# Expert layer of a decoder block: 39 padded tiles gathered and scattered, or 32 dense tiles read by 39 slots and summed in SBUF

## What is computed

```
logits = xf @ w_router.T                  # 2048 tokens x 8 experts
topw, topi = top_k(softmax(logits), 2)    # two experts for each token
topw = topw / sum(topw)
down_e = (silu(xf @ w_gate[e].T) * (xf @ w_up[e].T)) @ w_down[e].T
out = x + sum over its two experts of topw * down_e
```

## Time and profile before

| | |
|---|---|
| median of 3 runs | 475.76 us (475.4 to 476.47) |
| the profiled execution, its own time | 476.23 us |
| its span in the profile | 474.4 us |
| share of the span that PE / DVE / ACT / POOL are busy | 89% / 68% / 61% / 44% |
| mean granted clock of PE | 0.963 of full |

### The profile page before, as it was taken

One profiled execution on the slowest core, in us unless ns is written; L12 is line 12 of the kernel. 1 busy time (PEld: TensorE's weight loads), 2 busy tenths in 40 slices (PEclk: granted clock), 3 DMA queues, 4 the chain that ended last, 5 costly groups with the idle time before them and its releaser, 6 DMA issues. The chain is left out here.

```text
span 474.4 us, 13915 instructions
## 1 busy us (share of the span) xinstructions
PE 422.3 (89%) x4047; PEld 341.0 (72%) x4047; DVE 324.8 (68%) x969; ACT 291.1 (61%) x868; POOL 206.4 (44%) x482
## 2 busy tenths in 40 slices
PE   3989999999999999999988899987988999999950
PEld 3567777777777677777766687887877888888840
DVE  5579888888888888888885688888762333333325
ACT  4678888888888888888875877642022323323224
POOL 1545455454554554555531110100014777777740
PEclk9999999999999999999998999999778999999985
DMA  6363111111111111111000000001017766666526
GB/s 181 74 226 126 34 34 43 33 35 42 33 44 33 33 44 33 34 44 33 11 2 1 0 2 1 1 1 68 23 33 240 216 210 197 210 208 202 190 59 240
DMA packets 31999, 38.86 MB, mean 82 GB/s; under 512 B 5952, under 2 KB 29184, under 8 KB 31712
## 3 DMA queue, kind: packets, MB, share of 16 engines
q1 hardware_dynamic: 29040, 33.33, 22.9%
q0 software_dynamic: 2496, 5.12, 3.4%
q10 hardware_dynamic: 432, 0.02, 0.1%
HBM read 33.80 MB, written 4.65 MB: 81 GB/s over the span
## 5 line engine op out<-in xcount | busy, mean ns | idle before, releaser
L397 ACT ACTIVATE PR<-PS,nmax 128x257 f32<-128x257 f32 x256 | 117.9, 474 | 32.8 <-DVE nmax L582 32.7
L582 DVE TENSOR_REDUCE nmax<-PS 128x1 f32<-128x257 f32 x256 | 90.5, 416 | 17.5 <-PE PS L872 16.7
L879 PE MATMUL PS<-I,PR 128*128 128x128 f32 x512 | 67.3, 275 | 0.0
L346 POOL DMA_INDIRECT XG<-x_table,IDX x39 | 37.9, 971 | 57.4 <-DVE IDX L796 45.8
L879 PEld LDWEIGHTS PS<-I,PR 128*128 128x128 f32 x512 | 58.6, 142 | 0.3 <-issue 0.3
L300 POOL TENSOR_TENSOR O<-OM 128x64 f32<-128x64 f32 x64 | 20.4, 319 | 85.6 <-DVE OM L605 85.6
L802 DVE TENSOR_TENSOR H<-PS,SG 128x384 f32<-128x384 f32 x39 | 21.8, 558 | 50.9 <-PE PS L1089 50.9
L397 ACT ACTIVATION_READ_ACCUMULATOR PR<-PS,nmax 128x1 f32 x256 | 52.0, 203 | 0.0
L527 ACT ACTIVATE SG<-PS 128x384 f32<-128x384 f32 x39 | 19.1, 490 | 50.3 <-PE PS L1089 50.3
L894 PE MATMUL PS<-PT,KV 128*32 128x128 f32 x1024 | 41.6, 280 | 7.0 <-DVE PT L587 6.2
L872 PE MATMUL PS<-KV,QM 32*128 32x257 f32 x512 | 45.8, 427 | 1.3 <-ACT PR L397 0.7
(11 more groups left out here) (190 smaller groups left out, 836.5 us busy)
## 6 DMA issues: line engine op xcount, KB each, us to landing
CR<-ctxT SPq DMA_DIRECT2D x64, 128.0 KB, 2.1
GC<-w_gate SPq DMA_DIRECT2D x39, 192.0 KB, 2.7
UC<-w_up SPq DMA_DIRECT2D x39, 192.0 KB, 3.1
Y<-y_table SPq DMA_DIRECT2D x4, 512.0 KB, 5.1
DW<-w_down SPq DMA_DIRECT2D x1, 1536.0 KB, 6.0
NAMES<-lanes SPq DMA_DIRECT2D x1, 1344.0 KB, 9.1
X<-x SPq DMA_DIRECT2D x4, 256.0 KB, 4.6
x_table<-xe SPq DMA_DIRECT2D x4, 256.0 KB, 2.4
```

Source lines behind the costliest of these rows:

```text
L397: a.activation(PR[:, j % 2, gr, 0:S], src, ACT.Exp, bias=bias, accum_out=rsum[:, j % 2, gr:gr + 1]).then_inc(exped, 1)
L582: v.tensor_reduce(nmax[:, gr:gr + 1], bank[gr][:, 0:S], AX.X, ALU.max, negate=True).then_inc(max_ready, 1)
L879: ins = t.transpose(bank[4 + ch][:, 128 * gr:128 * gr + 128], PR[:, j % 2, gr, KC * ch:KC * ch + KC], I128[:, :])
```

## The change

The padding goes away. The 4096 pairs are sorted by expert without gaps, so they fill exactly `LT` = 32 tiles; a tile in which an expert ends and another begins belongs to both. The loop runs over `SLOTS` = 32 + 8 - 1 = 39 slots, each a pair of (tile, expert): the slot's expert comes out of `packed` as before, and its tile is the slot's number less the expert's (`tile_of`).

- POOL gathers 32 tiles and scatters 32. `XG` has 20 places, so 20 gathers come first; then gather t+20 and scatter t in turn, while gathers last, and scatters alone after that. Scatter t waits until slot t+7 is summed. Eight semaphores go round among the gathers.
- `XGT` keeps all 32 turned tiles, so gate and up read it at an address out of a register.
- A slot computes all 128 rows of its tile. DVE sets the rows of other experts to zero on the way out of PSUM (`own_rows`, a maximum and a minimum against `least` and `most` of that slot), and adds the tile to `YA` in SBUF (`added`), whose place is also an address out of a register. POOL zeroes `YA` beforehand. The scatter reads `YA`.
- The masks `least` and `most` are nine more instructions on DVE, behind `IDX` and ahead of the loop. DVE now also loads the five packed words into registers.
- The routing loses five DVE instructions (`over` to `base`) and the padding's `empty`; the places come out of PE ready for use. One `keep_busy` has 5 matmuls in place of 10.
- The two turns of tiles 0 and 1 both come ahead of the first gate product; after that a slot turns tile s+2.

```
-TILES = (2 * B * L + E * 127) // 128
-XRING, YRING, WRING = 4, 4, 4
+LT = 2 * B * L // 128
+SLOTS = LT + E - 1
+XRING, GRING, WRING = 20, 8, 4
...
-        owner_steps = 19
+        owner_steps = 13
         def owners_of(engine):
             _, words = nc.values_load_multi_w_load_instructions(packed[0:1, :], engines=[engine],
                                                                 min_val=0, max_val=E ** PER_WORD - 1)
-            return [((words[s // PER_WORD] >> (3 * (s % PER_WORD))) & (E - 1)) * IP for s in range(TILES)]
+            return [((words[s // PER_WORD] >> (3 * (s % PER_WORD))) & (E - 1)) for s in range(SLOTS)]
...
-            for n in range(YRING):
-                sp.wait_ge(scattered[n], 16 * len(range(n, TILES, YRING)))
+            sp.wait_ge(scattered, 16 * LT)
...
-            def gather(s):
-                g.indirect_dma_start(XG[:, s % XRING, :], None, x_table[:, :],
-                                     bass.IndirectOffsetOnAxis(IDX[:, s:s + 1], 0)).then_inc(gathered[s % XRING], 16)
+            def gather(t):
+                if t >= GRING:
+                    g.wait_ge(gathered[t % GRING], 16 * (t // GRING))
+                if t >= XRING:
+                    g.wait_ge(c["xg_turned"], t - XRING + 1)
+                g.indirect_dma_start(XG[:, t % XRING, :], None, x_table[:, :],
+                                     bass.IndirectOffsetOnAxis(IDX[:, t:t + 1], 0)).then_inc(gathered[t % GRING], 16)
+            def scatter(t):
+                g.wait_ge(c["ys"], t + E)
+                g.indirect_dma_start(y_table[:, :], bass.IndirectOffsetOnAxis(IDY[:, t:t + 1], 0),
+                                     YA[:, t, :], None).then_inc(scattered, 16)
+            g.memset(YA[:, :, :], 0.0).then_inc(c["ya_zeroed"], 1)
             g.wait_ge(c["x_stored"], 64)
-            g.wait_ge(c["ids"], 4)
-            for s in range(XRING):
-                gather(s)
-            for s in range(TILES):
-                if s + XRING < TILES:
-                    g.wait_ge(c["xg_turned"], s + 1)
-                    gather(s + XRING)
-                g.wait_ge(c["ys"], s + 1)
-                g.indirect_dma_start(y_table[:, :], bass.IndirectOffsetOnAxis(IDY[:, s:s + 1], 0),
-                                     YS[:, s % YRING, :], None).then_inc(scattered[s % YRING], 16)
+            g.wait_ge(c["ids"], 3)
+            for t in range(XRING):
+                gather(t)
+            for t in range(LT):
+                if t + XRING < LT:
+                    gather(t + XRING)
+                scatter(t)
...
-            def turned_rows(s):
-                a.wait_ge(c["xg_turned"], s + 1)
-                if s >= 2:
-                    a.wait_ge(c["up"], s - 1)
-                a.activation(XGT[:, s % 2, :], bank[6 + s % 2][:, 0:128], ACT.Copy).then_inc(c["xg_copied"], 1)
+            def turned_rows(t):
+                a.wait_ge(c["xg_turned"], t + 1)
+                a.activation(XGT[:, 128 * t:128 * t + 128], bank[6 + t % 2][:, 0:128], ACT.Copy).then_inc(c["xg_copied"], 1)
...
+            turned_rows(1)
+            for s in range(SLOTS):
                 gated(s)
-                if s + 1 < TILES:
-                    turned_rows(s + 1)
+                if s + 2 < LT:
+                    turned_rows(s + 2)
...
-            per_tile = bank[7][:, 0:E]
-            v.wait_ge(c["counted"], 1)
-            then(v.tensor_tensor(over[:, :, :], bc(per_tile.unsqueeze(2), [128, E, T]),
-                                 bc(parts["starts"].unsqueeze(1), [128, E, T]), ALU.is_gt))
-            then(v.tensor_reduce(tiles[:, :], over[:, :, :], AX.X, ALU.add))
-            then(v.tensor_tensor(before[:, :, :], bc(tiles[:, :].unsqueeze(1), [128, E, E]),
-                                 parts["lower"].rearrange("p (a b) -> p a b", a=E), ALU.mult))
-            then(v.tensor_reduce(begin[:, :], before[:, :, :], AX.X, ALU.add))
             v.wait_ge(c["placed"], 1)
-            counts_of = bank[5][:, 0:128].rearrange("p (t e) -> p t e", t=T)
-            then(v.scalar_tensor_tensor(out=base[:, :, :], in0=bc(begin[:, :].unsqueeze(1), [128, T, E]), scalar=128.0, in1=counts_of,
-                                        op0=ALU.mult, op1=ALU.add))
-            then(v.tensor_tensor(picked[:, :, :, :], OH[:, :, :, :], bc(base[:, :, :].unsqueeze(1), [128, 2, T, E]), ALU.mult))
+            place = bank[5][:, 0:128].rearrange("p (t e) -> p t e", t=T)
+            then(v.tensor_tensor(picked[:, :, :, :], OH[:, :, :, :], bc(place.unsqueeze(1), [128, 2, T, E]), ALU.mult))
...
+            v.memset(ownf[:, SLOTS:], 0.0).then_inc(c["masks"], 1)
+            then(v.tensor_tensor(starts[:, :], bank[6][:, 0:E - 1], parts["last"], ALU.min))
+            per_slot = [128, SLOTS, E - 1]
+            then(v.tensor_tensor(owner[:, :, :], bc(parts["slot_end"].unsqueeze(2), per_slot), bc(starts[:, :].unsqueeze(1), per_slot), ALU.is_gt))
+            then(v.tensor_reduce(ownf[:, 0:SLOTS], owner[:, :, :], AX.X, ALU.add))
+            then(v.tensor_tensor(ownf[:, 0:SLOTS], ownf[:, 0:SLOTS], parts["digits"], ALU.mult))
+            v.wait_ge(c["masks"], 1)
+            v.tensor_reduce(found[:, :], bank[7][:, 128:128 + 2 * LT].rearrange("p (a s) -> p s a", a=2), AX.X, ALU.add).then_inc(c["ids"], 1)
+            v.tensor_copy(IDY[:, :], found[:, :]).then_inc(c["ids"], 1)
+            v.tensor_scalar(IDX[:, :], IDY[:, :], 1, None, ALU.arith_shift_right).then_inc(c["ids"], 1)
+            k = [1]
+            def mask_step(ins):
+                k[0] += 1
+                ins.then_inc(c["masks"], 1)
+                v.wait_ge(c["masks"], k[0])
+            mask_step(v.tensor_tensor(bound[:, :, :], owner[:, :, :], bc(starts[:, :].unsqueeze(1), per_slot), ALU.mult))
+            mask_step(v.tensor_reduce(first_in[:, :], bound[:, :, :], AX.X, ALU.max))
+            mask_step(v.scalar_tensor_tensor(out=bound[:, :, :], in0=owner[:, :, :], scalar=BEYOND, in1=bc(starts[:, :].unsqueeze(1), per_slot),
+                                             op0=ALU.mult, op1=ALU.add))
+            mask_step(v.tensor_reduce(next_in[:, :], bound[:, :, :], AX.X, ALU.min))
+            mask_step(v.tensor_tensor(after_first[:, :], parts["position"], first_in[:, :], ALU.is_ge))
+            mask_step(v.scalar_tensor_tensor(out=before_next[:, :], in0=parts["position"], scalar=128.0, in1=next_in[:, :], op0=ALU.add, op1=ALU.is_lt))
+            mask_step(v.tensor_tensor(after_first[:, :], after_first[:, :], before_next[:, :], ALU.mult))
+            mask_step(v.tensor_scalar(most[:, :], after_first[:, :], BIG, None, ALU.mult))
+            mask_step(v.tensor_scalar(least[:, :], after_first[:, :], -BIG, None, ALU.mult))
...
+            def own_rows(s):
                 v.wait_ge(c["down"], s + 1)
-                if s >= YRING:
-                    v.wait_ge(scattered[s % YRING], 16 * (s // YRING))
-                v.tensor_copy(YS[:, s % YRING, :], bank[4 + s % 2][:, 0:D]).then_inc(c["ys"], 1)
-            for s in range(TILES):
+                if s >= 2:
+                    v.wait_ge(c["ys"], s - 1)
+                v.tensor_scalar(YS[:, s % 2, :], bank[4 + s % 2][:, 0:D], least[:, s:s + 1], most[:, s:s + 1],
+                                ALU.max, ALU.min).then_inc(c["own_rows"], 1)
+            def added(s, own):
+                v.wait_ge(c["own_rows"], s + 1)
+                if s >= 1:
+                    v.wait_ge(c["ys"], s)
+                tile = YA[:, bass.ds(tile_of(s, own), 1), :].rearrange("p t d -> p (t d)")
+                v.tensor_tensor(tile, YS[:, s % 2, :], tile, ALU.add).then_inc(c["ys"], 1)
+            v.wait_ge(c["ya_zeroed"], 1)
+            own = owners_of(mybir.EngineType.DVE)
+            for s in range(SLOTS):
                 multiplied(s)
                 if s >= 1:
-                    scaled(s - 1)
-            scaled(TILES - 1)
+                    own_rows(s - 1)
+                    added(s - 1, own[s - 1])
+            own_rows(SLOTS - 1)
+            added(SLOTS - 1, own[SLOTS - 1])
...
-            keep_busy(10, 0)
+            keep_busy(5, 0)
...
-            t.matmul(bank[7][:, 0:E], TOT[:, :], parts["per_expert"], start=True, stop=True).then_inc(c["counted"], 1)
-            t.matmul(bank[5][:, 0:128], TOT[:, :], parts["tile_earlier"], start=False, stop=True).then_inc(c["placed"], 1)
+            t.matmul(bank[5][:, 0:128], TOT[:, :], parts["places_before"], start=False, stop=True)
+            t.matmul(bank[6][:, 0:E - 1], TOT[:, :], parts["starts"], start=True, stop=True).then_inc(c["placed"], 1)
...
+            def gate_and_up(s, own):
+                t.wait_ge(c["xg_copied"], min(s + 1, LT))
...
+                        ins = t.matmul(bank[bk][:, 128 * n:128 * n + 128], w[:, s % WRING, 128 * n:128 * n + 128],
+                                       XGT[:, bass.ds(tile_of(s, own) * 128, 128)], start=True, stop=True)
...
-                    t.wait_ge(c["ys"], s - 1)
+                    t.wait_ge(c["own_rows"], s - 1)
...
```

(51 more changed lines are left out.)

69 lines of the change are left out of this document (26 added, 43 removed).

## The result

The changed kernel takes **460.12 us**, the median of four runs (459.48 to 461.85); the kernel before, beside it on the same chip, 476.12 (475.4 to 477.57). The ratio is 0.9695, with a 95% interval of 0.9665 to 0.9724: 16.0 us less. The profiled execution took 459.48 us with a span of 457.6, where 460.0 and 458.2 had been forecast for such a run. On the median's scale the forecast was 459.5, with a range of 457.5 to 468.0.

The account below looks back on a forecast made before the run. The prediction took POOL to bound the loop at 2.58 us a tile, PE 0.46 behind. Its terms, -15.17 - 1.9 + 0.53 + 0.32 = -16.2 us, gave 459.5 us on the median's scale, range 457.5 to 468.0.

Parts of the forecast that it names:

- The bound: Loop: POOL holds it at 2.58 us a tile; PE's pace of 2.12 would give 15.17 us.
- POOL's order: Loop: first scatter near 378, twelve pairs end at 409, then scatters catch up and the last, near 441.8, follows PE.
- Ahead of the loop: Routing before the loop: 1.9 us sooner in sum; then the order on PE makes slot 1 0.53 later.
- the sooner start: Routing, count's matmul behind MK: ten keep-busy passes fewer give 0.8 us, bounds 0 and 1.0.
- the half clock: Routing: fewer keep-busy matmuls may leave PE's clock at half on four passes, costing 0 to 0.5 us, taken as 0.25.
- The five DVE steps that went: Routing, between the end of the places and picked: their removal gives 1.1 us, 0.1 of handover staying.
- The turn ahead of gate 0: Loop start: gate 0 waits for the second gather, 1.28 to 3.42 us, taken as 1.46; net 0.53 later without copy waits.
- The nine mask steps: DVE between IDX and the first H: 5.3 us at most, hidden with 2 us to spare, register load included.
- Behind it: After the loop: masked copy replaces the copy and the sum is new, 0.32 us later; what follows the last scatter stays.
- A register block on PE: Rival, ahead of each gate product: 0.23 us in every slot gives 468.0, in half of them 463.8; chance 0.16.
- DVE's sum: Rival, every slot: sum waits for POOL's whole instruction, 478.1 us; chance of slower 0.04, of a partial hold 0.06.
- the third rival: POOL stays the bound in the loop if a DMA takes 1.41 us or more; 465 at 1.5; chance 0.07.

Follow-up runs that it names:

- before_ahead: The kernel before with 20 gathers ahead and a ring of 39 result places, all 78 indirect DMAs kept: 470.02 us.
- the extra pass: One more matmul of 128 columns per slot on PE, in both kernels: 469.72 us in the changed one, 477.27 in the one before.
- after_keep10: The changed kernel with ten keep-busy matmuls ahead of the count in place of five: 459.58 us.

## Why the prediction was right, point by point

**The bound.** POOL before, PE after, at 2.12 us a slot: shown by the chain, by `before_ahead` and by the extra pass in both kernels. The loop gave 14.90 us where the prediction had 15.17. Slot 1's gate alone is more than the 0.27 between them: at 1.21 us it still ran partly at half the clock and was priced at 0.83, which is 0.38; the other slots were 0.11 in all under the rounded 2.12 and 2.02.

**POOL's order.** The first scatter came at 377.7, forecast near 378; the last of the pairs began its scatter at 405.95 and was done at 406.9, forecast 409; the scatters caught up with the sums at 415.8, and the last one stood at 441.55, forecast 441.8. POOL does not hold the end, but it is not free of it either: the last scatter waited for scatter 30 in front of it (440.28 to 441.25).

**Ahead of the loop.** Of the 2.99 us, 0.54 lie ahead of anything that changed: `MK` starts at 338.25 against 338.79, and in the other executions of the changed kernel and its variants at 338.4 to 338.8, in variants of the old one at 339.1 and 340.0. From `MK` to `IDX` it is 2.45 where 1.9 was forecast, and the split was off. `MK` to `picked` gave 1.59. By `after_keep10` only 0.13 of that is the five matmuls: the sooner start, priced at 0.8, gave 0.92, but the half clock, priced at 0 to 0.5 and taken as 0.25, cost 0.79. The five DVE steps that went, priced at 1.1, so carry nearly all, 1.46. `found` to `IDX` without `empty` gave 0.27, forecast 0.23. The other 0.59 lies between `picked` and `found`, which was costed at nothing; 0.26 of it is a wait of `found` for PE, which this profile doesn't have. In the kernel before it reads:

```profile
351.33 0.24 DVE L790 TENSOR_REDUCE found<-PS 128x39 f32<-128x78 f32 x1 [0.26 <-PE PS L1074]
```

In other executions of the changed code that wait is longer, up to 1.27 (last section), and `MK` to `IDX` then gains as little as 1.2.

The turn ahead of gate 0 cost more than was taken: the second turn ran 2.09 after the first, between the 1.28 and 3.42 given, where 1.46 was taken. That the step came to 0.66 and not some 1.2 is owed to three things that stood in no term: the first gate and up were 0.22 faster here (2.50 against 2.72), gate 0 starts 0.17 behind the start of the second turn where a turn takes 0.33, and the first turn came 0.10 sooner behind `IDX`. Gates 0 and 1 no longer wait for ACT, as forecast.

The nine mask steps took from 349.18 to 352.24 and are hidden: `H` waited for PE for 6.64 us ahead of its first product. The 1.56 us by which the prediction priced the register load is no price for it, since its row names the landing of the gather as what ended it.

**Behind it.** The mis-sized term: "the last masked copy takes the place of the copy" priced it as a plain copy, 0.29, and it takes 0.41; together with scatter 30 on POOL the tail is 0.80 later, not 0.32. What follows the last scatter was costed at nothing and was 0.37 shorter. By the chain, 0.13 of it is SP's wait for the scatters, on four semaphores before and on one now (0.15 us against 0.02 from the landing to the read-back), and 0.21 is the read-back of `y_table`, 3.83 against 3.62 us. The four semaphores fit the other kernels too: the stretch took 16.4 us in both profiles that have them and 15.9 to 16.2 in the twelve with one, `before_ahead` (16.05) among them. Why the read-back itself differs is not shown.

**Luck.** That the sum of 16.2 came within 0.6 us of 16.8 is in part luck. The 0.54 ahead of `MK` and the 0.37 at the end stood in no term, and the routing in this execution was near the fast end of what the same code shows. What the runs bear out is the term that carries the forecast, the loop's 15.17.

**The rivals.** A register block on PE does show where the sequencer was not ahead (0.39 of the weight load's time at slot 1 with 32 places), and costs nothing in the steady loop: the reading of the earlier trace rows held, that of the earlier trace rows is the exception. DVE's sum was not held by POOL: 39 sums took 291 to 334 ns, the one at 398.31 within a scatter's time 0.29 us, the extra ones of the same size 280 to 314. The Trainium skill's rule (SBUF — State Buffer, section Who interferes with whom) of two SBUF inputs against a GpSimd instruction that reads SBUF is so not borne out for an indirect DMA; the same section also says, as inferred, that such a sum takes only the read part of the shared ports while descriptor generation needs the write part, which would fit, and which no run here tests. POOL's DMA stayed at 0.97 us, so the third rival had no start. Cover on DVE was some 0.65 us a slot by the estimate above (2.12 - 1.47), not 0.5: in the safe direction.

## What to carry to other kernels

Where an engine issues transfers in a fixed order, look first at whether that order makes each wait for the one before: reading 20 ahead gave about as much here (6.56 us) as dropping fourteen of the 78 transfers on top of it (6.88). Each without the other left time behind: 470.02 us with the order and all 78, 470.22 with 64 and only 12 ahead. Price independent instructions on the engine that isn't the bound by the distance between their starts, not by durations, and add up every wait it has in a slot before calling the room used. And price each new instruction by its own form: a copy that also clamps is not a copy.

## What the runs showed of the hardware that was not expected

- A masked copy out of PSUM (two clamps by a value per partition, 128x128) takes 410 ns; the plain copy of the same size 292 ns.
- Independent DVE instructions in a row start 0.08 to 0.09 us before the one ahead is recorded as done (0.46 to 0.47 us apart at 0.55 us long).
- The sum's wait for its register address is either 0.30 or 0.38 us behind the masked copy, in one and the same loop.
- The instant at which the clock rises differs between executions of the same code, and with it the routing. From `MK` to `IDX` (starts) the changed kernel and its variants with the same routing took 10.83 to 12.07 us. Windows and `found` on DVE, first of the changed kernel, then of the one with 32 places:

```profile
341.00:345.00 4.00, 4.00 (x30) 4.00 (x30) 3.76 (x13) 0.72 (x1) 0.00 (x0) 0.81 0.00 0
...
348.61 0.23 DVE L792 TENSOR_REDUCE found<-PS 128x32 f32<-128x64 f32 x1
```

```profile
341.00:345.00 4.00, 4.00 (x19) 4.00 (x20) 3.75 (x13) 0.72 (x1) 0.00 (x0) 0.50 0.00 0
...
350.02 0.23 DVE L792 TENSOR_REDUCE found<-PS 128x32 f32<-128x64 f32 x1 [1.27 <-PE PS L1100]
```

PE runs twelve keep-busy matmuls (24 passes) and then the place matmuls (L1100) in this stretch. With the clock at 0.81 they are done before DVE asks; at 0.50 DVE waits 1.27 us for them, and all that follows is later by it. With ten keep-busy matmuls (0.71 in the window of 338 to 341) the one execution took 10.98. Whether the five that were removed make the late rise more frequent stays open: one execution can't tell.
